# WKV recurrence with the distance to the past mean, two of its VectorE passes turned into ScalarE activations

## Chip, cores and metric

The kernel runs on one NeuronCore of a Trainium2 chip. The time is the device time in microseconds of one execution; medians are over repeated runs. PE is TensorE, DVE is VectorE, ACT is ScalarE, POOL is GpSimd, SP is SyncE.

## What is computed

Input x is 16 x 512 x 256 (8192 tokens, 256 channels), in fp32. After a layer norm there are two branches: `s`, an RWKV block (time mix and channel mix), and `g`, the SiLU of a mixture of 8 experts. The output is x + s * g. The part that the change touches is the time mix's recurrence:

```
def step(carry, kv_t):                  # one token, all channels
    aa, bb, pp = carry
    ww = u + kt
    p = jnp.maximum(pp, ww)
    e1 = jnp.exp(pp - p);  e2 = jnp.exp(ww - p)
    y = (e1 * aa + e2 * vt) / (e1 * bb + e2)
    ww2 = pp + w
    p2 = jnp.maximum(ww2, kt)
    e1 = jnp.exp(ww2 - p2);  e2 = jnp.exp(kt - p2)
    return ((e1 * aa + e2 * vt, e1 * bb + e2, p2), y)
rwkv = einsum(sigmoid(r) * y, Wo);  x = x + rwkv
```

Here w is minus the exponential of the decay parameter, u is `time_first`, and k, v, r are projections of the mixed tokens. The channel mix follows: relu squared of a 256 to 1024 projection, a projection back, gated by a sigmoid.

## The kernel before

The work has two stages. In the first, a round `b` takes one sequence of 512 tokens, channels on the partitions in two chunks `c` of 128 (`CH` = 2); there are 16 rounds, 0 to 15. In the second stage 72 tiles of 128 sorted tokens go through their expert.

Each engine has its own program with its instructions in an order written out by hand, and engines wait for each other on semaphores. An engine that waits holds up all that stands behind it in its program.

The recurrence is done by scans along the free dimension. In `wkv_start` DVE makes the running maximum `pp` (a scan), `qb` = pp - k, and in line 1317 the first exponent `E1` = min(qb + wneg, 0). ACT (`exponents`, `exps`) makes the second exponent `E2` with a Relu (line 562) and takes both exponentials (lines 566 and 568). `wkv_state` scans the denominator into `lb` (line 1323), `logs` takes its logarithm (line 574, with an ACT table load), `wkv_gap` adds it to `qb` (line 1330). `shares` then makes two tanh: that of the past in `E1` (line 580, with a table load) and that of now in `E2` (line 583). `wkv_mix` has seven DVE passes for each chunk: the share that is kept (line 1341), the fresh part (1344), the scan of the weighted mean `yy` (1348), 2v - mean (1353), and the three that join them and multiply by the receptance into `att` (1359, 1364, 1370).

A round of PE is, in order: `hidden(b-1)` (lines 845 to 852), `receptance(b-1)` in two halves (863), `channel_out(b-1, 0)` (875), `turn1(b+1)` (transposes, 780), `channel_out(b-1, 1)`, `project_out(b)` (827, reads `att`), `project(b+1, 0, 1)` (815, keys and values), `channel_out(b-1, 2)`, `turn2(b)`, `project(b+1, 2)`, `channel_out(b-1, 3)`. Between them stand small matmuls of the router.

ACT does in its round: the relus of `hidden` (596) and their squares (600), with `logs` after the second relu and `shares` after the sixth; then relus 6 and 7, three squares, the norm of the next sequence (510), two tanh (608), the affine after the transposes (518), copies of the projections (557, 555), the second norm (510), and at the end of the round for each chunk one copy, one exponent Relu (562) and one `split_mix` copy into `mix_hi` (589), then `exps`. The second half of `receptance` waits for relu 6, `channel_out(b-1, 0)` for all squares, `hidden(b)` for both copies into `mix_hi`.

On DVE `wkv_mix` is followed by a piece of routing work, `mix1(b+1)` (1277, 1282), `residual1` (1399, which waits for `project_out`; the second projection chunk of PE waits for it in turn), `wkv_start(b+1)`, `mix2` and `wkv_state` of the next round. In rounds 0 to 3 DVE also makes the router's statistics and softmax, in 11 it chooses the expert of each token, in 12 it places the tokens; from round 12 on POOL scatters list rows by indirect DMAs (line 400), which stand ahead of the scales of the next norm (lines 407 to 412) in its program.

Of the kernel before, what the change touches and what calls it, by code (L numbers as in the profile page):

```python
# [29 lines left out]
ALU = mybir.AluOpType  # L30
ACT = mybir.ActivationFunctionType
# [3 lines left out]
P = 128  # L35
# [6 lines left out]
WKV_STEPS = 16  # L42
PARAMS = ["ln1_w", "ln1_b", "ln2_w", "ln2_b", "decay", "first", "tmk", "tmv", "tmr", "cmk", "cmr"]


# [23 lines left out]
def rwkv_times_moe(nc, x, xT, vec, ln0_w, ln0_b, WkT, WvT, WrT, WoT, WfkT, WfrT, WfvT, Wg, W1, W2,  # L69
                   consts, tile_iota, token_ids, pad_rows, sorted_list, xs_rows, out):  # L70
    T, C = x.shape
    SEQ = 512
    NB = T // SEQ
    CH = C // P
    J = SEQ // P
# [3 lines left out]
    E, _, F = W1.shape  # L79
# [9 lines left out]
    with ExitStack() as ctx:  # L89
        def sb(name, shape, dt=F32):  # L90
            return ctx.enter_context(nc.sbuf_tensor(name, shape, dt))
# [7 lines left out]
        V = {n: i for i, n in enumerate(PARAMS)}  # L99
        wneg = sb("wneg", [P, CH])  # L100
        half_w = sb("half_w", [P, CH])
        half_u = sb("half_u", [P, CH])
        w0_bc = sb("w0_bc", [P, C])
        b0_bc = sb("b0_bc", [P, C])
# [42 lines left out]
        yy = [part(SEQ + 1) for _ in range(CH)]  # L147
# [6 lines left out]
        x_in = part(J * C).rearrange("p (j c) -> p j c", j=J)  # L154
# [67 lines left out]
        state_done log_done gap_done past_done now_done  # L222
# [5 lines left out]
        S = {n: sem(n) for n in names}  # L228
# [262 lines left out]
        def _(act):  # L491
# [67 lines left out]
            def exponents(b, c):  # L559

                wait_run(act, S["pre_done"], b * CH + (c + 1))
                act.activation(E2[:, c], qb[c], ACT.Relu, bias=wneg[:, c:c + 1]).then_inc(S["relu2_done"], 1)

            def exps(b):

                act.activation(E1, E1, ACT.Exp).then_inc(S["exp_done"], 1)
                wait_run(act, S["relu2_done"], b * CH + CH)
                act.activation(E2, E2, ACT.Exp, scale=-1.0).then_inc(S["exp_done"], 1)

            def logs(b):  # L570
# [5 lines left out]
            def shares(b):  # L576

                for c in range(CH):
                    wait_run(act, S["gap_done"], b * CH + (c + 1))
                    act.activation(E1[:, c], qb[c], ACT.Tanh, scale=-0.5, bias=half_w[:, c:c + 1]  # L580
                                   ).then_inc(S["past_done"], 1)
                for c in range(CH):
                    act.activation(E2[:, c], qb[c], ACT.Tanh, scale=-0.5, bias=half_u[:, c:c + 1]
                                   ).then_inc(S["now_done"], 1)
# [396 lines left out]
        def _(v):  # L981

            v.memset(hT[:, :, 0:1], 0.0)
            for c in range(CH):
                v.memset(pp[c][:, 0:1], -1e38)
                v.memset(lb[c][:, 0:1], 0.0)
                ins = v.memset(yy[c][:, 0:1], 0.0)
            ins.then_inc(S["columns_set"], 1)
            v.wait_ge(S["columns_set"], 1)

            def decay_parts():
                v.wait_ge(S["decay_exp"], 1)
                v.tensor_scalar(half_w[:], wneg[:], 0.5, None, ALU.mult)
                v.tensor_scalar(wneg[:], wneg[:], -1.0, None, ALU.mult)
                v.tensor_scalar(half_u[:], vecs[:, :, V["first"]], 0.5, None, ALU.mult)

            def prepare():
                v.wait_ge(S["weights_in"], 16 * 4)
                v.tensor_scalar(wo.rearrange("p k n -> p (k n)"), wo.rearrange("p k n -> p (k n)"), 0.125, None, ALU.mult)
# [304 lines left out]
            def wkv_start(b):  # L1304

                st = Steps(v, S["wkv_step"], WKV_STEPS, b, S["waited"])
                for c in range(CH):
                    v.wait_ge(S["kvr_ready"], b * (3 * CH) + (c + 1))
                    st.then(v.tensor_tensor_scan(pp[c][:, 1:SEQ + 1], wneg[:, c:c + 1].to_broadcast([P, SEQ]),
                                                 kvs[:, 0, c, :], -1e38, ALU.add, ALU.max))  # L1310
                for c in range(CH):
                    st.wait(1 + c)
                    st.then(v.tensor_tensor(qb[c], pp[c][:, 0:SEQ], kvs[:, 0, c, :], ALU.subtract))

                for c in range(CH):
# [16 lines left out]
            def wkv_mix(b):  # L1332

                st = Steps(v, S["wkv_step"], WKV_STEPS, b, S["waited"])
                st.k = 2 * CH
                val, r = kvs[:, 1], kvs[:, 2]
                v.wait_ge(S["kvr_ready"], b * (3 * CH) + 3 * CH)
                kept, fresh = [], []
                for c in range(CH):
                    wait_run(v, S["past_done"], b * CH + (c + 1))  # L1340
                    kept.append(st.then(v.tensor_scalar(pp[c][:, 1:SEQ + 1], E1[:, c], -0.5, 0.5, ALU.mult, ALU.add)))
                for c in range(CH):
                    st.wait(kept[c])
                    fresh.append(st.then(v.scalar_tensor_tensor(E1[:, c], E1[:, c], 1.0, val[:, c], ALU.add, ALU.mult)))
                means = []
                for c in range(CH):
                    st.wait(fresh[c])
                    means.append(st.then(v.tensor_tensor_scan(yy[c][:, 1:SEQ + 1], pp[c][:, 1:SEQ + 1], E1[:, c],
                                                              0.0, ALU.mult, ALU.add)))
                news = []  # L1350
                for c in range(CH):
                    st.wait(means[c])
                    news.append(st.then(v.scalar_tensor_tensor(val[:, c], val[:, c], 2.0, yy[c][:, 0:SEQ],
                                                               ALU.mult, ALU.subtract)))
                wait_run(v, S["now_done"], b * CH + CH)
                steps_to = []
                for c in range(CH):
                    st.wait(news[c])
                    steps_to.append(st.then(v.scalar_tensor_tensor(E2[:, c], E2[:, c], 1.0, val[:, c],
                                                                   ALU.add, ALU.mult)))  # L1360
                sums = []
                for c in range(CH):
                    st.wait(steps_to[c])
                    sums.append(st.then(v.scalar_tensor_tensor(E2[:, c], yy[c][:, 0:SEQ], 2.0, E2[:, c],
                                                               ALU.mult, ALU.add)))
# [227 lines left out]
```

## Time and profile before

| | before |
|---|---|
| median of 3 runs | 1146.2 us (1146.09 to 1147.34) |
| profiled execution | 1145.82 us, of which its span is 1144.0 us |
| busy share of the span: PE, DVE, ACT, POOL | 92%, 77%, 55%, 31% |
| first stage (rounds) | up to about 850 us |
| one of the rounds 5 to 10 | 47.5 us |
| granted TensorE clock, mean | 0.98 of full speed |

The span is from the first to the last instruction of the profile. Busy shares are means over stages with different limits; idle time of an engine counts only where another one waits for its result. A row with [t <-engine tile line] had t us of idle time on its engine just ahead of it, which that instruction ended. Rows with a count merge several instructions; their time is from the start of the first to the end of the last.

### The profile page before, as it was taken

What the parts mean: (1) busy time and instruction counts of PE and PEld (TensorE: products, weight loads), DVE (VectorE), ACT (ScalarE), POOL (GpSimd) and SP (SyncE); (2) the same over time, 40 slices, a digit from 0 to 9 for tenths busy, and PEclk for the clock granted to TensorE, in tenths of its full rate; (3) what the DMA queues carried; (4) which work ended last, traced back from release to release, by engine and by line L of the source; (5) the groups of instructions that cost most, each with busy time, mean ns of one, the idle gap of its engine ahead of it and who ended that gap; (6) DMA issues with size and microseconds to landing.
All of it is one profiled execution on the core that took longest, in us unless ns stands there. A gap on an engine that the chain in (4) does not pass through costs nothing.

```text
span 1144.0 us, 19481 instructions
## 1 busy us (share of the span) xinstructions
PE 1056.0 (92%) x5152; PEld 835.4 (73%) x5153; DVE 878.3 (77%) x1988; ACT 627.6 (55%) x1085; POOL 353.9 (31%) x403
## 2 busy tenths in 40 slices
PE   5689999999999999999998698989899999999997
PEld 5358777677766777767775577667788888888886
DVE  5899797988989889898898868786426666666664
ACT  2647466685765857658574557647333333433332
POOL 3122313100001000010000537364406555555563
PEclk9889999999999999999999899999999999999999
DMA  9422230110101101011010101053503333323220
GB/s 305 159 89 93 92 110 0 38 47 10 55 0 55 55 0 55 0 55 55 1 56 1 56 1 56 1 184 107 204 19 107 91 95 97 102 90 97 88 75 15
DMA packets 60054, 80.44 MB, mean 70 GB/s; under 512 B 7774, under 2 KB 47327, under 8 KB 60002
## 3 DMA queue, kind: packets, MB, share of 16 engines
q1 hardware_dynamic: 48658, 54.69, 14.7%
q0 software_dynamic: 11360, 25.32, 7.3%
q8 instruction: 17, 0.28, 0.1%
q14 instruction: 19, 0.16, 0.0%
HBM read 65.17 MB, written 26.49 MB: 80 GB/s over the span
## 4 chain that ended last, share of the span: by engine, by line
PE 55%; DVE 14%; issue 14%; ACT 11%; POOL 4%; DMA 1%; DVEq 1%; ACTq 0%; SPq 0%; POOLq 0%
PE psM L946 11%; PE psM L815 11%; PE psKV L875 11%; PE psM L957 5%; PE psR L957 5%; ACT arena L596 3%; PE psM L827 3%; DVE arena L1282 2%; POOL sorted_list L400 2%; PE psT L780 2%; ACT arena L600 2%; PE psT L936 2%; PE psR L736 2%; ACT L580 1%; ACT L574 1%
## 5 line engine op out<-in xcount | busy, mean ns | idle before, releaser
L875 PE MATMUL psKV<-arena 128*128 128x256 f32 x1024 | 236.0, 384 | 3.4 <-ACT arena L600 1.7
L875 PEld LDWEIGHTS psKV<-arena 128*128 128x128 f32 x1024 | 193.8, 192 | 42.6 <-issue 14.8
L815 PE MATMUL psM<-arena 128*128 128x512 f32 x384 | 174.2, 600 | 1.0
L407 POOL TENSOR_SCALAR lnw<-mv 128x4 f32<-128x4 f32 x32 | 8.8, 275 | 484.5 <-DVE mv L1263 484.3
L946 PE MATMUL psM<-arena 128*128 128x128 f32 x1152 | 144.3, 279 | 0.1
L946 PEld LDWEIGHTS psM<-arena 128*128 128x128 f32 x1152 | 135.8, 193 | 4.2 <-issue 1.8
L690 ACT ACTIVATE arena<-arena,info_t 128x256 f32<-128x256 f32 x72 | 43.1, 600 | 161.9 <-DVE info_t L1441 153.6
L815 PEld LDWEIGHTS psM<-arena 128*128 128x128 f32 x384 | 70.7, 192 | 81.7 <-issue 80.1
L467 POOL DMA_INDIRECT out_dram<-arena,out_idx x72 | 88.5, 1229 | 95.8 <-DVE row_idx L1436 81.9
L1282 DVE SCALAR_TENSOR_TENSOR arena<-arena,vecs 128x512 f32<-128x512 f32 x160 | 108.7, 746 | 0.0
L845 PE MATMUL psM<-mix_hi,wfk_hi 128*128 128x512 f32 x256 | 103.6, 405 | 2.5 <-ACT mix_hi L589 1.3
L510 ACT ACTIVATE arena<-s_ring,cf 128x256 f32 (+1 forms) x128 | 66.3, 591 | 68.0 <-POOL cf L412 68.0
L400 POOL DMA_INDIRECT sorted_list<-info_cur,place_cur x64 | 71.1, 1111 | 97.5 <-DVE info_cur L1239 78.6
L557 ACT ACTIVATE arena<-psM 128x512 f32<-128x512 f32 x64 | 36.5, 588 | 115.6 <-PE psM L815 115.6
L847 PE MATMUL psM<-mix_hi,wfk_lo 128*128 128x512 f32 x256 | 99.9, 390 | 0.0
L596 ACT ACTIVATE arena<-psM 128x512 f32<-128x512 f32 x128 | 74.1, 590 | 38.2 <-PE psM L852 38.0
L863 PE MATMUL psM<-arena 128*128 128x256 f32 x256 | 64.5, 396 | 24.5 <-ACT arena L596 24.5
L518 ACT ACTIVATE arena<-psT,vecs 128x512 f32<-128x512 f32 x64 | 46.4, 774 | 68.6 <-PE psT L780 68.6
L1507 DVE COPY arena<-arena 128x1024 f32 x72 | 50.4, 700 | 43.7 <-issue 41.7
L1277 DVE TENSOR_TENSOR arena<-arena 128x512 f32<-128x512 f32 x64 | 42.6, 692 | 53.3 <-ACT arena L518 53.3
L852 PE MATMUL psM<-mix_lo,wfk_hi 128*128 128x512 f32 x256 | 79.2, 390 | 0.7 <-DVE mix_lo L1301 0.7
L600 ACT ACTIVATE arena<-arena 128x512 f32<-128x512 f32 x128 | 77.1, 626 | 0.0
(191 smaller groups left out, 2006.4 us busy)
## 6 DMA issues: line engine op xcount, KB each, us to landing
desk<-in_x SPq DMA_DIRECT2D x16, 512.0 KB, 5.0
arena<-in_x SPq DMA_DIRECT2D x16, 512.0 KB, 3.8
desk<-in_xT SPq DMA_DIRECT2D x16, 512.0 KB, 4.1
xs_rows<-s_ring SPq DMA_DIRECT2D x16, 512.0 KB, 3.2
xs_rows<-in_x SPq DMA_DIRECT2D x16, 512.0 KB, 4.3
desk<-in_W SPq DMA_DIRECT2D x8, 512.0 KB, 8.3
arena<-in_W SPq DMA_DIRECT2D x8, 512.0 KB, 7.5
out_dram<-arena,out_idx POOLq DMA_INDIRECT x72, 2.8
```

What stands on the lines that cost most here:

```text
L400: pool.indirect_dma_start(sorted_list[:, :], bass.IndirectOffsetOnAxis(place_cur[:, j:j + 1], axis=0), info_cur[:, j, :], None).then_inc(S ...
L467: pool.indirect_dma_start(out[:, :], bass.IndirectOffsetOnAxis(out_idx[i][:, 0:1], axis=0), out_t[i], None, bounds_check=T - 1, oob_is_err ...
L596: act.activation(kf2[:, h], psM[:, h % 3, :], ACT.Relu).then_inc(S["relu_done"], 1)
L600: act.activation(kf2[:, h], kf2[:, h], ACT.Square).then_inc(S["sq_done"], 1)
L815: ins = pe.matmul(psM[:, u % 3, :], w[:, k, c * P:(c + 1) * P], mixA[:, m, k, :], start=(k == 0), stop=(k == CH - 1))
L845: pe.matmul(psM[:, h % 3, :], wfk_hi[:, k, n], mix_hi[:, k, :], start=(k == 0), stop=False)
L847: pe.matmul(psM[:, h % 3, :], wfk_lo[:, k, n], mix_hi[:, k, :], start=False, stop=False)
L852: ins = pe.matmul(psM[:, h % 3, :], wfk_hi[:, k, n], mix_lo[:, k, :], start=False, stop=(k == CH - 1))
L875: ins = pe.matmul(psKV[:, j // 2, (j % 2) * C:(j % 2 + 1) * C], kf2[:, h, j * P:(j + 1) * P], wfv[:, h, :], start=(h == 0), stop=(h == HC ...
L946: ins = pe.matmul(psM[:, i % 2, f * P:(f + 1) * P], w1_t[i % 2][:, k, f * P:(f + 1) * P], xnT[i % 2][:, k, :], start=(k == 0), stop=(k == ...
L957: ins = pe.matmul(y_ps[i % 2], hT_t[i % 2][:, f, :], w2_sb[:, ds(w + f * C, C)], start=(f == 0), stop=(f == FK - 1))
L1282: ins = v.scalar_tensor_tensor(dst[:, c], dmix[:, c], vecs[:, c, V[m]:V[m] + 1], hT[:, c, 0:SEQ], ALU.mult, ALU.add)
```

## The change

The recurrence is written with the distance of the token's value to the mean of the past: `wkv_mix` takes differences of neighbouring values and scans them into `lb`, weighted by the kept share; five DVE passes for each chunk instead of seven. The kept share is made by ACT from the past tanh (`kept_done`), ahead of the tanh of now. The first exponent is made in two steps by ACT, as Relu(wpos - qb) and a negative scale in the exponential, instead of line 1317 on DVE. `yy` goes, `x_in` takes its place in SBUF, two small constants (`wpos`, `half_c`) are added, and the scale of `wo` becomes 0.25.

```
             def exponents(b, c):
                 wait_run(act, S["pre_done"], b * CH + (c + 1))
                 act.activation(E2[:, c], qb[c], ACT.Relu, bias=wneg[:, c:c + 1]).then_inc(S["relu2_done"], 1)
+                act.activation(E1[:, c], qb[c], ACT.Relu, scale=-1.0, bias=wpos[:, c:c + 1]).then_inc(S["relu2_done"], 1)
             def exps(b):
-                act.activation(E1, E1, ACT.Exp).then_inc(S["exp_done"], 1)
-                wait_run(act, S["relu2_done"], b * CH + CH)
+                wait_run(act, S["relu2_done"], b * (2 * CH) + 2 * CH)
+                act.activation(E1, E1, ACT.Exp, scale=-1.0).then_inc(S["exp_done"], 1)
                 act.activation(E2, E2, ACT.Exp, scale=-1.0).then_inc(S["exp_done"], 1)
...
             def shares(b):
...
                     act.activation(E1[:, c], qb[c], ACT.Tanh, scale=-0.5, bias=half_w[:, c:c + 1]
                                    ).then_inc(S["past_done"], 1)
+                for c in range(CH):
+                    wait_run(act, S["past_done"], b * CH + (c + 1))
+                    act.activation(pp[c][:, 1:SEQ + 1], E1[:, c], ACT.Identity, scale=-0.5, bias=half_c[:, 0:1]
+                                   ).then_inc(S["kept_done"], 1)
                 for c in range(CH):
                     act.activation(E2[:, c], qb[c], ACT.Tanh, scale=-0.5, bias=half_u[:, c:c + 1]
                                    ).then_inc(S["now_done"], 1)
...
             def wkv_start(b):
...
-                    st.then(v.tensor_tensor(qb[c], pp[c][:, 0:SEQ], kvs[:, 0, c, :], ALU.subtract))
-
-                for c in range(CH):
-                    st.wait(3 + c)
-                    v.tensor_scalar(E1[:, c], qb[c], wneg[:, c:c + 1], 0.0, ALU.add, ALU.min).then_inc(S["pre_done"], 1)
+                    v.tensor_tensor(qb[c], pp[c][:, 0:SEQ], kvs[:, 0, c, :], ALU.subtract).then_inc(S["pre_done"], 1)
...
             def wkv_mix(b):
...
-                    kept.append(st.then(v.tensor_scalar(pp[c][:, 1:SEQ + 1], E1[:, c], -0.5, 0.5, ALU.mult, ALU.add)))
...
-                    fresh.append(st.then(v.scalar_tensor_tensor(E1[:, c], E1[:, c], 1.0, val[:, c], ALU.add, ALU.mult)))
...
-                    news.append(st.then(v.scalar_tensor_tensor(val[:, c], val[:, c], 2.0, yy[c][:, 0:SEQ],
-                                                               ALU.mult, ALU.subtract)))
+                for c in range(CH):
+                    wait_run(v, S["kept_done"], b * CH + (c + 1))
+                    steps.append(st.then(v.tensor_tensor(E1[:, c, 1:SEQ], val[:, c, 1:SEQ], val[:, c, 0:SEQ - 1],
+                                                         ALU.subtract)))
...
+                    dist.append(st.then(v.tensor_tensor_scan(lb[c][:, 1:SEQ + 1], pp[c][:, 0:SEQ], E1[:, c],
+                                                             0.0, ALU.mult, ALU.add)))
...
+                    back.append(st.then(v.scalar_tensor_tensor(E2[:, c], E2[:, c], -1.0, lb[c][:, 1:SEQ + 1],
+                                                               ALU.add, ALU.mult)))
...
+                    sums.append(st.then(v.scalar_tensor_tensor(E2[:, c], val[:, c], 2.0, E2[:, c],
                                                                ALU.mult, ALU.add)))
```

## Rows read from the trace of the kernel before

**Rows 1.** page, section 1: busy time of each engine

```profile
PE 1056.0 (92%) x5152; PEld 835.4 (73%) x5153; DVE 878.3 (77%) x1988; ACT 627.6 (55%) x1085; POOL 353.9 (31%) x403
```

**Rows 2.** waits of the matmul engine over the span (total us, times, longest us)

```profile
PE psM L863 <- ACT arena L596: 24.5, 13, 5.3
```

**Rows 3.** timeline of ACT in round 8 (start, duration, line, tiles, count)

```profile
439.38 1.33 ACT L580 ACTIVATE arena<-arena,half_w 128x512 f32<-128x512 f32 x2
440.62 1.32 ACT L583 ACTIVATE arena<-arena,half_u 128x512 f32<-128x512 f32 x2
441.84 1.06 ACT L596 ACTIVATE arena<-psM 128x512 f32<-128x512 f32 x2
442.80 1.66 ACT L600 ACTIVATE arena<-arena 128x512 f32<-128x512 f32 x3
...
449.29 1.45 ACT L518 ACTIVATE arena<-psT,vecs 128x512 f32<-128x512 f32 x2 [1.90 <-PE psT L780]
```

**Rows 4.** timeline of PE in round 8

```profile
442.47 1.99 PE L863 MATMUL psM<-arena 128*128 128x256 f32 x8 [1.52 <-ACT arena L596]
444.60 3.69 PE L875 MATMUL psKV<-arena 128*128 128x256 f32 x16
...
456.05 7.50 PE L815 MATMUL psM<-arena 128*128 128x512 f32 x16
```

**Rows 5.** timeline of PE in round 13

```profile
714.27 7.03 PE L815 MATMUL psM<-arena 128*128 128x512 f32 x16
```

**Rows 6.** timeline of DVE in round 8

```profile
441.03 0.76 DVE L1341 TENSOR_SCALAR arena<-arena 128x512 f32<-128x512 f32 x2
...
445.16 1.27 DVE L1353 SCALAR_TENSOR_TENSOR arena<-arena 128x512 f32<-128x512 f32 x2
...
451.62 1.29 DVE L1277 TENSOR_TENSOR arena<-arena 128x512 f32<-128x512 f32 x2
...
456.80 1.21 DVE L1399 TENSOR_TENSOR s_ring<-s_ring,psM 128x1024 f32 x1
```

**Rows 7.** groups of instructions: the first exponent on DVE

```profile
L1317 DVE TENSOR_SCALAR arena<-arena,wneg 128x512 f32<-128x512 f32 x32 | 14.0, 479 | 0.0
```

**Rows 8.** timelines of ACT, DVE and PE at the end of round 8

```profile
472.19 0.71 ACT L562 ACTIVATE arena<-arena,wneg 128x512 f32<-128x512 f32 x1
472.81 0.62 ACT L589 ACTIVATE mix_hi<-arena 128x512 fp32r<-128x512 f32 x1
...
475.35 2.34 DVE L1323 TENSOR_TENSOR_SCAN arena<-arena 128x512 f32<-128x512 f32 x2 [1.10 <-ACT arena L568]
...
474.96 0.48 PE L845 MATMUL psM<-mix_hi,wfk_hi 128*128 128x512 f32 x1
```

**Rows 9.** timeline of PE: waits of the other rounds

```profile
86.04 0.47 PE L845 MATMUL psM<-mix_hi,wfk_hi 128*128 128x512 f32 x1 [0.51 <-ACT mix_hi L589]
...
204.73 1.99 PE L863 MATMUL psM<-arena 128*128 128x256 f32 x8 [1.78 <-ACT arena L596]
...
610.03 2.07 PE L768 MATMUL psR<-desk,cst 128*128 128x512 f32 x2 [4.09 <-DVE desk L1170]
...
706.46 1.06 PE L780 MATMUL psT<-cst,arena 128*128 128x128 f32 x8 [1.50 <-ACT arena L510]
...
802.36 3.72 PE L827 MATMUL psM<-arena 128*128 128x256 f32 x16 [1.44 <-DVE arena L1370]
```

**Rows 10.** timeline of POOL in round 13

```profile
689.16 1.09 POOL L400 DMA_INDIRECT sorted_list<-info_cur,place_cur  x1 [15.52 <-DVE info_cur L1239]
```

**Rows 11.** timeline of PE around a stall in the expert stage

```profile
856.09 1.95 PE L946 MATMUL psM<-arena 128*128 128x128 f32 x16
...
862.09 0.44 PE L936 MATMUL psT<-cst,arena 128*128 128x128 f32 x2 [2.32 <-ACT arena L690]
862.36 3.52 PE L946 MATMUL psM<-arena 128*128 128x128 f32 x16
```

**Rows 12.** window after that stall (busy us by engine, PEclk, DMA share, GB/s)

```profile
862.60:863.00 0.40, 0.40 (x4) 0.40 (x3) 0.40 (x3) 0.28 (x1) 0.40 (x1) 0.50 0.70 236
```

More of the change, by code:

```diff
@@ L41 @@
 R_PEXP, R_COUNTS, R_SEL, R_ONEHOT, R_KEPT, R_ALL = 9, 13, 18, 30, 31, 54
-WKV_STEPS = 16
+WKV_STEPS = 10
 PARAMS = ["ln1_w", "ln1_b", "ln2_w", "ln2_b", "decay", "first", "tmk", "tmv", "tmr", "cmk", "cmr"]
@@ L101, in rwkv_times_moe @@
         half_w = sb("half_w", [P, CH])
+        wpos = sb("wpos", [P, CH])
+        half_c = sb("half_c", [P, 1])
         half_u = sb("half_u", [P, CH])
@@ L146, in rwkv_times_moe @@
         lb = [part(SEQ + 1) for _ in range(CH)]
-        yy = [part(SEQ + 1) for _ in range(CH)]
+        x_in = part(J * C).rearrange("p (j c) -> p j c", j=J)
         att = part(CH * SEQ).rearrange("p (c t) -> p c t", c=CH)
@@ L153, in rwkv_times_moe @@
         moe_end = at[0]
-        x_in = part(J * C).rearrange("p (j c) -> p j c", j=J)
         mixB_r = part(CH * SEQ).rearrange("p (c t) -> p c t", c=CH)
@@ L221, in rwkv_times_moe @@
         h1_ready mix1_step mix1_done mixr1_done proj_done kvr_ready wkv_step pre_done relu2_done exp_done att_done o_done
-        state_done log_done gap_done past_done now_done
+        state_done log_done gap_done past_done kept_done now_done
         x2_done ln2_step ln2_stats cf2_ready hn2_ready tr2_done h2_ready mix2_step mixk_done mixk_hi wfk_hi_done mix2_done mixr2_done
@@ L983, in _ @@
             v.memset(hT[:, :, 0:1], 0.0)
+            v.memset(half_c[:], 0.5)
             for c in range(CH):
                 v.memset(pp[c][:, 0:1], -1e38)
-                v.memset(lb[c][:, 0:1], 0.0)
-                ins = v.memset(yy[c][:, 0:1], 0.0)
+                ins = v.memset(lb[c][:, 0:1], 0.0)
             ins.then_inc(S["columns_set"], 1)
@@ L993, in decay_parts @@
                 v.tensor_scalar(half_w[:], wneg[:], 0.5, None, ALU.mult)
+                v.tensor_copy(wpos[:], wneg[:])
                 v.tensor_scalar(wneg[:], wneg[:], -1.0, None, ALU.mult)
@@ L998, in prepare @@
                 v.wait_ge(S["weights_in"], 16 * 4)
-                v.tensor_scalar(wo.rearrange("p k n -> p (k n)"), wo.rearrange("p k n -> p (k n)"), 0.125, None, ALU.mult)
+                v.tensor_scalar(wo.rearrange("p k n -> p (k n)"), wo.rearrange("p k n -> p (k n)"), 0.25, None, ALU.mult)
                 v.tensor_scalar(wfv.rearrange("p k n -> p (k n)"), wfv.rearrange("p k n -> p (k n)"), 0.5, None,
@@ L1334, in wkv_mix @@
                 st = Steps(v, S["wkv_step"], WKV_STEPS, b, S["waited"])
-                st.k = 2 * CH
+                st.k = CH
                 val, r = kvs[:, 1], kvs[:, 2]
                 v.wait_ge(S["kvr_ready"], b * (3 * CH) + 3 * CH)
-                kept, fresh = [], []
+                steps = []
                 for c in range(CH):
-                    wait_run(v, S["past_done"], b * CH + (c + 1))
-                    kept.append(st.then(v.tensor_scalar(pp[c][:, 1:SEQ + 1], E1[:, c], -0.5, 0.5, ALU.mult, ALU.add)))
+                    wait_run(v, S["kept_done"], b * CH + (c + 1))
+                    steps.append(st.then(v.tensor_tensor(E1[:, c, 1:SEQ], val[:, c, 1:SEQ], val[:, c, 0:SEQ - 1],
+                                                         ALU.subtract)))
@@ L1342, in wkv_mix @@
+                dist = []
                 for c in range(CH):
-                    st.wait(kept[c])
-                    fresh.append(st.then(v.scalar_tensor_tensor(E1[:, c], E1[:, c], 1.0, val[:, c], ALU.add, ALU.mult)))
-                means = []
-                for c in range(CH):
-                    st.wait(fresh[c])
-                    means.append(st.then(v.tensor_tensor_scan(yy[c][:, 1:SEQ + 1], pp[c][:, 1:SEQ + 1], E1[:, c],
-                                                              0.0, ALU.mult, ALU.add)))
@@ L1350, in wkv_mix @@
-                news = []
-                for c in range(CH):
-                    st.wait(means[c])
-                    news.append(st.then(v.scalar_tensor_tensor(val[:, c], val[:, c], 2.0, yy[c][:, 0:SEQ],
-                                                               ALU.mult, ALU.subtract)))
[L1355 to L1360, printed above, removed]
+                    st.wait(steps[c])
@@ new lines, in wkv_mix @@
+                    dist.append(st.then(v.tensor_tensor_scan(lb[c][:, 1:SEQ + 1], pp[c][:, 0:SEQ], E1[:, c],
+                                                             0.0, ALU.mult, ALU.add)))
+                wait_run(v, S["now_done"], b * CH + CH)
+                back = []
+                for c in range(CH):
+                    st.wait(dist[c])
+                    back.append(st.then(v.scalar_tensor_tensor(E2[:, c], E2[:, c], -1.0, lb[c][:, 1:SEQ + 1],
+                                                               ALU.add, ALU.mult)))
@@ L1361, in wkv_mix @@
                 sums = []
                 for c in range(CH):
-                    st.wait(steps_to[c])
-                    sums.append(st.then(v.scalar_tensor_tensor(E2[:, c], yy[c][:, 0:SEQ], 2.0, E2[:, c],
+                    st.wait(back[c])
+                    sums.append(st.then(v.scalar_tensor_tensor(E2[:, c], val[:, c], 2.0, E2[:, c],
                                                                ALU.mult, ALU.add)))
```

## The prediction

> **What bounds the kernel now.** I read the shares on the page first. PE is busy for 92% [rows 1], so only its idle time can be won, and any new idle time of PE is lost. The next view is the list of PE's waits. Beside waits at the kernel's ends, the largest group is the matmul of `receptance` (L863) that waits for ACT's relu (L596): 24.5 us in 13 waits, the longest 5.3 [rows 2], one in each of the rounds 3 to 15.
>
> Then one round's timelines, round 8, which stands for the rounds 4 to 10 (47.5 us each). ACT runs without a pause from the past tanh over the now tanh, relus 6 and 7, three squares and on to the norm [rows 3]. PE's second half of `receptance` starts at 442.47, after 1.52 us idle, just when relu 6 is done (442.3 to 442.4), and `channel_out` at 444.60, just after the last square (442.80 + 1.66 = 444.46) [rows 3, 4]. So this stretch of ACT's chain is on the path. PE then runs on to `project`, whose 16 matmuls take 7.50 us; in round 13, where `residual1` isn't late, they take 7.03 [rows 4, 5]. The 0.47 us are the second wait of the round: `residual1` starts at 456.80, after `mix1`, though PE was done with `project_out` at about 456.05 [rows 4, 6]. That one belongs to DVE.
>
> **The sum, part by part.** All is counted against the profiled execution's 1145.8 us; the median is 0.4 higher.
>
> *DVE's removed passes.* Kept share: two passes, 441.03 to the start of the next group at 441.70, 0.67 us. The fresh part is replaced by a subtraction of the same size, at nothing. 2v - mean: two of 0.6 each, 1.19. The first exponent: two passes of 0.48, some 0.8 with their overlap [rows 6, 7]. That is 2.65 us a round off DVE, but two other things set when DVE's results are used. `mix1` (L1277, at 451.62) needs the affine of ACT (L518, 449.29 to 450.74 for both chunks), which comes later by what ACT is delayed, and `residual1` needs `project_out`. In rounds 4 to 10 the whole worth of the relief is the 0.47 us of `project`; it comes back in full, since `mix1` starts no later than 451.5 and `residual1` then starts when `project_out` ends.
>
> *ACT's added Identity passes.* Two of 128x512, ahead of the tanh of now, so ahead of relus 6 and 7 and the squares. The trace has no Identity of this shape from SBUF with a bias operand. The nearest rows: tanh with a bias starts every 0.62 us (439.38, 440.62, 441.84 with two each); a square without a bias every 0.52 (442.80 to 444.35 with three); the affine from PSUM, with two operands, 1.45 for two, at most 0.7 each [rows 3]. Bounds 1.04 to 1.4 a round; I take the tanh's, 1.24, since source, size and bias are alike. They need no wait: the tanh before them is done. All of it lands on PE, since relu 6 and the last square were both last to come. Queued behind them on ACT are also the norm and the affine of the next sequence, later by 1.24 like PE itself.
>
> *ACT's added Relus*, one for each chunk at the end of the round, 0.62 each (L562 at 472.19, next start 472.81). The second copy into `mix_hi` ended at 473.43 and `hidden` started at 474.96 [rows 8]. So 1.24 of the 1.5 us of cover are used up, and I cost it at nothing; without cover it would be up to 1.24 a round. The exponentials end later too, so DVE's scan (475.35) starts about 1.1 later. In rounds 4 to 10 DVE catches up in its wait for the logarithm; in rounds 12 to 14 it isn't hidden, since PE waits there for the norm (706.46, 1.50), whose scales stand on POOL behind DMAs that start on what DVE copies after that scan (689.16, after 15.52 idle) [rows 9, 10].
>
> *Round by round.*
> - Round 0: DVE ahead of `project_out` gains 1.0 (1.86 less 0.85 from later exponentials), but `hidden` waited there for `mix_hi` already (86.04, 0.51) [rows 9], which comes 1.2 later: +0.2 (an estimate from the same passes).
> - Rounds 1 and 2: no wait of `project` to give back: +1.24 each, 2.5.
> - Round 3: its `project` gives back 0.26: +1.0.
> - Rounds 4 to 10: 7 x (1.24 - 0.47) = +5.4.
> - Round 11: PE waits 4.09 for DVE's choice (610.03) [rows 9]. DVE comes to `residual1` 0.5 later, since `project_out` is later by 1.24 and it had been late by 0.7: +0.5.
> - Rounds 12 to 14: POOL's start, 1.1 each: +3.3. The 1.24 on ACT vanishes in the wait for the norm.
> - Round 15: PE waited 1.44 for `att` (802.36) [rows 9]; DVE's shorter mix takes that away, and ACT's 1.24 takes its place: -0.2.
>
> Together +12.7 us from the instruction times alone: 1158.5 in this execution's terms, 1158.9 as a median. With the Identity's bounds it is 11 to 14.
>
> *The clock.* Each of these stalls grows: 1.52 to 2.8 us in the rounds 4 to 10, 1.78 (204.73, the same in 13 to 15) to 3.0 [rows 9]. None of those up to 1.78 is followed by a lower clock. The one stall in the trace that lies near the new length, 2.32 us at 862.09 in the expert stage, is: the granted clock is 0.50 in the window after it, which is the 1.2 GHz level, and 16 matmuls that took 1.95 us before take 3.52, so 1.57 are lost [rows 11, 12]. The 4.09 us of round 11 also cost a fall. Whether one of 2.8 brings a fall each time the rows can't say; one row for it, none of its length against it; the 12 stalls up to 1.78 are shorter. I take half of the ten stalls whose loss would reach PE's end (3 to 11 and 15; in 13 and 14 the wait for the norm hides most): 5 x 1.57 = +7.9, with bounds 0 and 10 x 1.57 = 15.7. Sum: 12.7 + 7.9 = 20.6, so 1166.4, as a median **1166.8**.
>
> The Trainium skill (TensorE: Matmul & The Clock Gate, A second HAM failure mode: psum-queue depth-cycling) says that a PE that idles briefly and often between its groups goes back and forth between the two clocks and loses throughput. By that, all ten would come and the time would be near 1174. The 12 stalls up to 1.78 disagree with it, the one of 2.32 agrees.
>
> The same notes (ScalarE: Activation LUTs, Rules for kernel authors) say to put relu, add and multiply on VectorE, not on ScalarE, which speaks against this change. The rows agree: the kept share takes 0.33 us a chunk on DVE, a pass with a bias 0.62 on ACT.
>
> **Rivals.**
> - *The clock stays up* (a stall of 2.8 isn't enough, or falls into a good moment nearly always): 12.7 alone, about 1159. For it: seven rounds with 1.5 idle each keep the clock. Chance 0.24.
> - *It falls nearly each time*: 12.7 + 15.7 = 28.4, so 1174 to 1175. Chance 0.11.
> - *ACT's passes are hidden and DVE's relief counts*: faster. ACT has idle time in each round (1.90 ahead of L518 [rows 3]), and if relu 6 weren't held up, DVE would give 7 x 0.47, 0.3 in round 3, 1.0 in round 0, about 0.7 in round 11 and up to 1.4 in round 15: 6.7, so 1139.5. It decides from an Identity cost below 0.24 us each (0.47 a round for two); the shortest ACT row of this size takes 0.52. Chance 0.04.
> - *Within 0.2%*: the same with the Identity at about 0.3 each. Chance 0.03.
>
> **How the numbers follow.** Half of the falls, give or take three of them (1162 to 1172), holds 0.58. A measurement of this kernel tells 0.2%, 2.3 us, from no change. Range: from the case without falls, at the Identity's lower bound (1157), to nearly all falls (1175); outside are left about 0.13. Faster 0.04, within 0.2% 0.03, slower 0.93.
>
> **What would show it.** In the profile after: two Identity rows of about 0.62 between the tanh of L580 and of now; PE's wait for L596 at 2.7 to 3.1 us in rounds 3 to 10; `project` at 7.0 us; rounds 4 to 10 at 48.3 us without a fall and 49.9 with one; a granted clock of 0.5 for some matmuls of `channel_out` in about half of the rounds. DVE's busy time falls by some 40 us (2.65 x 16) and ACT's rises by about 45 (four passes of 0.71 x 16). It would be wrong if PE's wait for relu 6 stays at 1.5 (the Identities hidden), if `hidden` begins to wait for `mix_hi` (the Relus not hidden), or if the clock does other than half.

## The result

| | before | after |
|---|---|---|
| median | 1146.77 us (1146.09 to 1148.85, 4 runs) | 1169.58 us (1166.86 to 1175.80, 4 runs) |
| profiled execution, its span | 1145.82, 1144.0 us | 1170.22, 1168.4 us |
| mean granted TensorE clock | 0.98 | 0.97 |

The ratio is 1.0203 (95%: 1.016 to 1.0247): the change makes the kernel 2% slower. The forecast was 1166.8 us.

Page of the kernel after, busy time of each engine:

```profile
PE 1067.1 (91%) x5152; PEld 843.5 (72%) x5153; DVE 839.2 (72%) x1892; ACT 665.4 (57%) x1149; POOL 356.6 (31%) x403
```

Against [rows 1] DVE has 39.1 us less to do and ACT 37.8 more, so the work has moved as written. PE has the same number of matmuls and is busy for 11.1 us longer: some of them ran slower. The other 13.3 us of the longer span (24.4) are new idle time of PE, in sum over all its waits.

Waits of PE in the kernel after (total us, times, longest us):

```profile
PE psM L869 <- ACT arena L602: 43.7, 15, 7.5
...
PE psM L833 <- DVE arena L1366: 3.3, 1, 3.3
...
PE psM L851 <- ACT mix_hi L595: 2.4, 2, 1.6
```

The matmul of `receptance` (now L869) waits for the relus (now L602) for 43.7 us where it was 24.5 [rows 2]. No other group of waits grew like it; taken together the others shrank by 5.9 us. Where this comes from is in the timeline of ACT in round 7 of the kernel after (round 8 in [rows 3]; the rounds 4 to 10 are alike):

```profile
404.64 1.33 ACT L582 ACTIVATE arena<-arena,half_w 128x512 f32<-128x512 f32 x2
405.88 1.32 ACT L586 ACTIVATE arena<-arena,half_c 128x512 f32<-128x512 f32 x2
407.10 1.32 ACT L589 ACTIVATE arena<-arena,half_u 128x512 f32<-128x512 f32 x2
408.33 1.05 ACT L602 ACTIVATE arena<-psM 128x512 f32<-128x512 f32 x2
409.29 1.66 ACT L606 ACTIVATE arena<-arena 128x512 f32<-128x512 f32 x3
...
439.34 0.71 ACT L564 ACTIVATE arena<-arena,wpos 128x512 f32<-128x512 f32 x1
439.95 0.62 ACT L595 ACTIVATE mix_hi<-arena 128x512 fp32r<-128x512 f32 x1
```

The chain is still without a pause, and the two Identity passes (L586) take 1.22 us of it, from 405.88 to 407.10. Relu 6 starts 3.69 us after the past tanh, where it was 2.46. PE in the same round:

```profile
408.96 2.00 PE L869 MATMUL psM<-arena 128*128 128x256 f32 x8 [2.78 <-ACT arena L602]
411.09 3.71 PE L881 MATMUL psKV<-arena 128*128 128x256 f32 x16
...
422.57 7.11 PE L821 MATMUL psM<-arena 128*128 128x512 f32 x16
...
441.13 0.48 PE L851 MATMUL psM<-mix_hi,wfk_hi 128*128 128x512 f32 x1
```

The stall grew from 1.52 to 2.78 us. `project` takes 7.11 where it took 7.50 [rows 4], and `hidden` starts without a wait: the Relus (L564) are covered here. DVE in this round:

```profile
416.61 1.36 DVE L1284 TENSOR_TENSOR arena<-arena 128x512 f32<-128x512 f32 x2 [1.03 <-ACT arena L519]
...
422.83 1.22 DVE L1395 TENSOR_TENSOR s_ring<-s_ring,psM 128x1024 f32 x1 [0.89 <-PE psM L833]
```

DVE is now early: `residual1` (L1395) waited 0.89 us for `project_out`. What DVE gained beyond the 0.39 of `project` it spends waiting.

Round 5 shows the second part of the loss, the clock. PE's timeline, and below it four windows of it (busy us of PE, PEld, DVE, ACT and POOL, then PEclk, DMA share, GB/s):

```profile
310.73 2.76 PE L869 MATMUL psM<-arena 128*128 128x256 f32 x8 [2.78 <-ACT arena L602]
...
313.29 4.59 PE L881 MATMUL psKV<-arena 128*128 128x256 f32 x16
```

```profile
310.70:311.70 1.00, 0.97 (x4) 0.86 (x5) 1.00 (x2) 1.00 (x3) 0.00 (x0) 1.00 1.05 292
311.90:312.90 1.00, 1.00 (x4) 0.73 (x4) 1.00 (x3) 1.00 (x3) 0.00 (x0) 0.50 0.96 280
312.90:313.90 1.00, 1.00 (x4) 0.82 (x3) 1.00 (x3) 1.00 (x3) 0.00 (x0) 0.50 0.42 107
315.30:316.30 1.00, 1.00 (x6) 0.86 (x6) 0.70 (x5) 0.35 (x1) 0.00 (x0) 1.00 0.24 84
```

The same stall of 2.78 us, but a good microsecond after its end the granted clock is 0.50 (the 1.2 GHz level), and it is back at 2.4 GHz at 315.30. The two groups of matmuls take 7.35 us together instead of 5.71. Of the 15 rounds from 1 on, this profile shows such a fall after the stall in 3, 5, 8, 11, 13 and 14 (in 12, where a longer wait ends, before had one too).

Where the 24.4 us of span lie, from the times at which the same instructions start in the two profiles:

| stretch | longer by | made of |
|---|---|---|
| start to `hidden(0)` (86.04 to 88.53) | 2.5 | 0.5 ahead of `project_out(0)`, 0.9 of lower clock in it, 1.08 longer wait for `mix_hi` |
| to the stall of round 3 (204.73 to 212.28) | 5.1 | 3 x 1.24 and one fall (in round 0, after `hidden`) |
| to the stall of round 11 (585.07 to 604.10) | 11.5 | 8 x 0.92 and three falls at 1.30 |
| to the stall of round 12 (643.16 to 666.68) | 4.5 | 1.24, DVE late by 2.0, one fall |
| to the end | 0.9 | nearly all hidden |

In the rounds 4 to 10 a round without a fall takes 48.46 us (47.54 before) and one with a fall 49.76.

The first row of the table needs more than the page. In round 0 DVE's scan has to wait for the exponentials (L570), which in the kernel before were done when it started at 42.77; PE waits longer for DVE's next result (L742, 7.54 us where it was 6.48), and then less for `att` (L833, 3.26 where it was 5.13). DVE and PE of the kernel after, and `project_out(0)` of the kernel before:

```profile
45.17 2.34 DVE L1326 TENSOR_TENSOR_SCAN arena<-arena 128x512 f32<-128x512 f32 x2 [1.90 <-ACT arena L570]
...
50.93 3.56 PE L742 MATMUL psR<-desk 128*128 128x8 f32 x16 [7.54 <-DVE desk L1041]
...
64.28 6.27 PE L833 MATMUL psM<-arena 128*128 128x256 f32 x16 [3.26 <-DVE arena L1366]
```

```profile
63.76 5.39 PE L827 MATMUL psM<-arena 128*128 128x256 f32 x16 [5.13 <-DVE arena L1370]
```

The 16 matmuls of `project_out(0)` take 0.9 us longer because the clock, which is low there in both kernels, rises later: between 67.30 and 69.00 it is 0.50 in the kernel after and 1.00 in the kernel before.

### The profile page after: what moved, and what is told of

It reads as the page before. It is cut to its first block, busy times and chain, and to the rows that moved or that the text cites. A ratio compares the mean times of both kernels' runs of the same rounds, so it can differ in the third digit from the quotient of the medians.

```text
span 1168.4 us, 19401 instructions
## 1 busy us (share of the span) xinstructions
PE 1067.1 (91%) x5152; PEld 843.5 (72%) x5153; DVE 839.2 (72%) x1892; ACT 665.4 (57%) x1149; POOL 356.6 (31%) x403
## 4 chain that ended last, share of the span: by engine, by line
PE 68%; ACT 14%; issue 9%; DVE 4%; POOL 4%; DMA 1%; ACTq 0%; SPq 0%; POOLq 0%; DVEq 0%
PE psKV L881 17%; PE psM L821 13%; PE psM L952 11%; PE psM L963 5%; PE psR L963 5%; PE psM L833 5%; ACT arena L602 3%; PE psM L869 3%; PE psT L786 3%; POOL sorted_list L401 2%; PE psT L942 2%; PE psR L742 2%; ACT L582 1%; ACT L576 1%; ACT arena L606 1%
## 5 line engine op out<-in xcount | busy, mean ns | idle before, releaser
L881 PE MATMUL psKV<-arena 128*128 128x256 f32 x1024 | 242.3, 390 | 2.7 <-ACT arena L606 1.7
L881 PEld LDWEIGHTS psKV<-arena 128*128 128x128 f32 x1024 | 198.3, 197 | 44.2 <-issue 13.2
L952 PEld LDWEIGHTS psM<-arena 128*128 128x128 f32 x1152 | 134.3, 192 | 4.5 <-issue 2.1
L821 PEld LDWEIGHTS psM<-arena 128*128 128x128 f32 x384 | 71.7, 193 | 78.7 <-issue 77.9
L468 POOL DMA_INDIRECT out_dram<-arena,out_idx x72 | 92.6, 1287 | 91.2 <-DVE row_idx L1432 76.4
L869 PE MATMUL psM<-arena 128*128 128x256 f32 x256 | 70.0, 421 | 43.7 <-ACT arena L602 43.7
L869 PEld LDWEIGHTS psM<-arena 128*128 128x128 f32 x256 | 50.4, 205 | 56.8 <-ACT arena L602 49.8
L602 ACT ACTIVATE arena<-psM 128x512 f32<-128x512 f32 x128 | 74.2, 591 | 26.1 <-PE psM L858 26.1
```

Of the source, the lines that this page charges most:

```text
L468: pool.indirect_dma_start(out[:, :], bass.IndirectOffsetOnAxis(out_idx[i][:, 0:1], axis=0), out_t[i], None, bounds_check=T - 1, oob_is_err ...
L602: act.activation(kf2[:, h], psM[:, h % 3, :], ACT.Relu).then_inc(S["relu_done"], 1)
L821: ins = pe.matmul(psM[:, u % 3, :], w[:, k, c * P:(c + 1) * P], mixA[:, m, k, :], start=(k == 0), stop=(k == CH - 1))
L869: ins = pe.matmul(psM[:, (HC + u) % 3, (j % 2) * C:(j % 2 + 1) * C], mixB_r[:, k, j * P:(j + 1) * P], wfr[:, k, :], start=(k == 0), stop=( ...
L881: ins = pe.matmul(psKV[:, j // 2, (j % 2) * C:(j % 2 + 1) * C], kf2[:, h, j * P:(j + 1) * P], wfv[:, h, :], start=(h == 0), stop=(h == HC ...
L952: ins = pe.matmul(psM[:, i % 2, f * P:(f + 1) * P], w1_t[i % 2][:, k, f * P:(f + 1) * P], xnT[i % 2][:, k, :], start=(k == 0), stop=(k == ...
```

## The experiments

Eleven runs were made, in three groups, each group on one chip. There the kernel before took 1155 to 1160 us instead of 1147. In its one profile from there (before_again) the rounds 4 to 10 take 47.54 us as in the first, and 7.3 of the 9.0 us that its span is longer lie behind the stall of round 15, nearly all of that in the expert stage. So each kernel is read as a ratio to the kernel before on its own chip.

| kernel | median us | before there | ratio (95%) | rounds 4 to 10, no fall |
|---|---|---|---|---|
| kept_act | 1177.28 | 1159.89 | 1.0163 (1.0139 to 1.0188) | |
| exp_act | 1166.66 | 1159.89 | 1.0074 (1.0052 to 1.0097) | 47.71 |
| dist_only | 1155.22 | 1159.89 | 0.9959 (0.9941 to 0.9977) | 47.23 |
| filled | 1175.01 | 1159.89 | 1.0147 (1.0129 to 1.0165) | 48.44 |
| after_again | 1178.84 | 1154.58 | 1.0214 (1.0196 to 1.0232) | |
| now_late | 1157.27 | 1154.58 | 1.0011 (1.0000 to 1.0022) | 47.30 |
| dist_now_late | 1142.06 | 1154.58 | 0.9886 (0.9868 to 0.9903) | 46.35 |
| before_now_late | 1155.43 | 1154.58 | 1.0007 (0.9995 to 1.0018) | 47.54 |
| before_again | 1154.83 (one execution) | 1155.38 | | 47.54 |
| exp_again | 1162.27 | 1155.38 | 1.0069 (1.0050 to 1.0088) | 47.71 |
| kept_one | 1159.02 | 1155.38 | 1.0034 (1.0022 to 1.0047) | 47.78 |

### The three parts, each alone

**kept_act**: the kernel before, with only the kept share on ACT.

```
                                    ).then_inc(S["past_done"], 1)
+                for c in range(CH):
+                    wait_run(act, S["past_done"], b * CH + (c + 1))
+                    act.activation(pp[c][:, 1:SEQ + 1], E1[:, c], ACT.Identity, scale=-0.5, bias=half_c[:, 0:1]
+                                   ).then_inc(S["kept_done"], 1)
...
-                    wait_run(v, S["past_done"], b * CH + (c + 1))
-                    kept.append(st.then(v.tensor_scalar(pp[c][:, 1:SEQ + 1], E1[:, c], -0.5, 0.5, ALU.mult, ALU.add)))
...
+                    wait_run(v, S["kept_done"], b * CH + (c + 1))
```

> The kernel before with the kept share alone made by ACT (two Identity passes ahead of the tanh of now); DVE makes six passes per chunk, the first exponent stays on DVE. Theory (the Identities push relu 6 and the last square, and the longer stall brings clock falls): PE's wait for relu 6 grows from 1.5 to 2.8 us in rounds 4 to 10, a round there from 47.5 to 48.4; +10 to 11 us from the instruction times and about five falls of 1.3, so +14 to +20, about 1164. Rival (the cost sits in the Relus of the exponent and the later exponentials): +4 or less, under 1151.

**exp_act**: the kernel before, with only the first exponent on ACT (a Relu for each chunk, a negative scale in the exponential).

```
                 act.activation(E2[:, c], qb[c], ACT.Relu, bias=wneg[:, c:c + 1]).then_inc(S["relu2_done"], 1)
+                act.activation(E1[:, c], qb[c], ACT.Relu, scale=-1.0, bias=wpos[:, c:c + 1]).then_inc(S["relu2_done"], 1)
...
-                    st.wait(3 + c)
-                    v.tensor_scalar(E1[:, c], qb[c], wneg[:, c:c + 1], 0.0, ALU.add, ALU.min).then_inc(S["pre_done"], 1)
```

> The kernel before with the first exponent alone moved to ACT (two Relus at the end of the round, line 1317 gone). Theory: in rounds 1 to 11 the Relus hide behind PE (cover of 1.5 us ahead of hidden, 1.24 used), so nothing there; about +1.2 in round 0 where hidden waits for mix_hi, +1.1 in each of rounds 12 to 14 through POOL's start: +3 to +6, about 1151, and no new stall of PE above 1.8 us in rounds 3 to 10. Rival (half of the loss comes from here): +10 or more, and PE waits for mix_hi in every round.

**dist_only**: the kernel after, with the kept share and the first exponent back on DVE; only the new form of the recurrence is left.

```
-                for c in range(CH):
-                    wait_run(act, S["past_done"], b * CH + (c + 1))
-                    act.activation(pp[c][:, 1:SEQ + 1], E1[:, c], ACT.Identity, scale=-0.5, bias=half_c[:, 0:1]
-                                   ).then_inc(S["kept_done"], 1)
...
-                    wait_run(v, S["kept_done"], b * CH + (c + 1))
+                    wait_run(v, S["past_done"], b * CH + (c + 1))
+                    kept.append(st.then(v.tensor_scalar(pp[c][:, 1:SEQ + 1], E1[:, c], -0.5, 0.5, ALU.mult, ALU.add)))
```

> The changed kernel with the kept share and the first exponent back on DVE, so the new recurrence alone, which takes one pass per chunk (1.2 us a round) off DVE and adds nothing to ACT. Theory: project no longer waits for residual1 in rounds 4 to 10 (7 x 0.4), round 0 and round 15 gain 1.2 each, round 11 some 0.7: -5 to -7, about 1140, with PE's wait for relu 6 at 1.5 as before. Rival (DVE off the path altogether): within 1 us of before. Rival (DVE is the bound of the round): -1.2 x 15 = -18.

Measured: kept_act +18.7 us (1.63% of 1146.8), exp_act +8.5, dist_only -4.7. They sum to 22.5, where the whole gave 23.3 and, as after_again, 24.5; each of the three is known to some 2 to 3 us by its interval, so the sum fits. So the kept share on ACT is most of the loss, and the new form by itself is a small gain. kept_act and dist_only came out about as expected (dist_only a little short of its 5 to 7), exp_act cost more than the 3 to 6 us expected. PE in round 5 of kept_act, with the clock window after it:

```profile
306.74 3.37 PE L868 MATMUL psM<-arena 128*128 128x256 f32 x8 [2.77 <-ACT arena L601]
```

```profile
307.00:308.00 1.00, 1.00 (x3) 0.82 (x4) 1.00 (x2) 1.00 (x3) 0.00 (x0) 0.50 0.94 227
```

The stall is the same as in the kernel after, so it comes from the Identities alone. The clock fell after 10 of the 12 long stalls (rounds 3 to 11 and 13 to 15), more often than in the kernel after and twice as often as I had expected for this run. PE in round 5 of dist_only:

```profile
300.97 2.00 PE L864 MATMUL psM<-arena 128*128 128x256 f32 x8 [1.51 <-ACT arena L597]
...
314.59 7.11 PE L816 MATMUL psM<-arena 128*128 128x512 f32 x16
```

Here the stall stays at 1.51, and the shorter DVE gives back what it can: `project` takes 7.11 instead of 7.50, and the round 0.31 less.

### Does the clock count apart from the stall?

**filled**: the kernel after, where PE does the first half of `receptance` twice, the second time in what was idle time. The matmuls that wait for relu 6 can't start sooner.

```
                     pe.wait_ge(S["relu_done"], b * HC + (HC + u - 2))
-                    for j in (2 * u, 2 * u + 1):
+                    for j in (0, 1, 0, 1) if u == 0 else (2, 3):
```

> The changed kernel in which PE makes the first half of receptance twice, the same 8 matmuls again into the same bank, 1.9 us of work set into the wait for relu 6 (which ends when it ended before). The instruction times stay, but PE is idle for 0.9 instead of 2.8 us; in rounds 1 and 2, where the wait is only 1.2, it costs 0.7 each. Theory (the long idle stretch of PE is what lowers the clock): no falls in rounds 3 to 10, a time 4 to 8 us below the changed kernel, about 1164, and the spread from run to run gets small. Rival (the falls have another cause): the falls stay and the time is 1 to 2 us above the changed kernel.

**after_again**: the kernel after once more, on another chip.

> The changed kernel itself, beside the three reorderings on one chip. Theory and rival alike: about 2% slower than before (1.016 to 1.025), with PE waiting 2.7 to 3.0 us for relu 6 in rounds 3 to 11 and a fall of the clock in some of them, not in the same rounds as in the first profile.

PE in round 5 of filled, with the clock window around it:

```profile
308.90 2.00 PE L869 MATMUL psM<-arena 128*128 128x256 f32 x8 [1.04 <-ACT arena L602]
```

```profile
308.00:310.00 2.00, 1.10 (x5) 1.00 (x6) 2.00 (x2) 2.00 (x5) 0.00 (x0) 1.00 1.02 314
```

The rounds take 48.44 us, those of the kernel after without a fall 48.46. So in these rounds the added matmuls cost nothing and gain nothing in instruction times. No stall of the rounds 3 to 11 and 13 to 15 is followed by a fall, and the ratio is 1.0147 instead of 1.0203 and 1.0214: 0.6 to 0.7%, 6 to 8 us, are the clock's. The spread between runs, which I had expected to shrink clearly, was 3.6 us in 5 runs, against 6.6 in 12 runs of the kernel before there and 4.6 in 5 runs of after_again; with so few runs it settles nothing. In after_again the clock fell after 8 of the 12 long stalls, in other rounds than in the first profile (4, 7 to 10 and 13 to 15).

### Undoing the order instead of the work

**now_late**: the kernel after, with ACT's tanh of now moved behind relus 6 and 7 and the squares. ACT does the same work.

```
+            def share_now(b):
                 for c in range(CH):
                     act.activation(E2[:, c], qb[c], ACT.Tanh, scale=-0.5, bias=half_u[:, c:c + 1]
...
                     relus(b - 1, 6, 7)
                     squares(b - 1, 5, 6, 7)
+                share_now(b)
```

> The changed kernel with one move: ACT makes relus 6 and 7 and the squares 5, 6, 7 before the tanh of now, so the same ACT passes, two of them later. Theory (what costs is that the Identities stand ahead of relu 6 and the squares): PE's wait for relu 6 is back at 1.5 us, no falls in rounds 3 to 10, a round there 47.2 us, and what is left of the loss is round 0 and rounds 12 to 14: 1.000 to 1.005 of before. Rival (ACT's total time or DVE's wait for the kept share costs): little changes, above 1.012.

**dist_now_late**: the same move in dist_only.

> The new recurrence with kept share and first exponent on DVE, and the tanh of now after the squares. Theory: the last square ends 1.24 us earlier than in the kernel before, the wait for relu 6 falls to 0.3, and with 1.2 us less on DVE mix1 keeps pace: rounds 4 to 10 at 46.2 to 46.4 us, 0.985 to 0.990 of before. Rival (PE's wait only moves elsewhere): 0.995 or more, as the new recurrence alone.

**before_now_late**: the same move in the kernel before.

> The kernel before with only that move of the tanh of now. Theory: PE gets 1.2 us earlier to project, but mix1 and residual1 on DVE end when they did, so the wait of project for residual1 grows from 0.5 to 1.6 us and eats it: within 0.3% of before, rounds at 47.4 to 47.6. Rival (ACT's order is all that counts): as much as the move gives elsewhere, 0.99 or less.

PE in the stall of round 5, in now_late, in dist_now_late and in before_now_late:

```profile
303.58 2.00 PE L872 MATMUL psM<-arena 128*128 128x256 f32 x8 [1.53 <-ACT arena L604]
```

```profile
294.71 2.00 PE L867 MATMUL psM<-arena 128*128 128x256 f32 x8 [0.32 <-ACT arena L599]
```

```profile
298.36 1.99 PE L866 MATMUL psM<-arena 128*128 128x256 f32 x8 [0.29 <-ACT arena L598]
...
315.27 5.39 PE L818 MATMUL psM<-arena 128*128 128x512 f32 x12 [1.36 <-DVE s_ring L1402]
```

In now_late, with every added pass still on ACT, the stall is back at 1.53, no clock falls in the rounds 3 to 10, and of the 2.1% there are 0.11% left. ACT's work is the same as in the kernel after, so what costs is how much of it stands ahead of relu 6, not how much ACT does in all. The added passes have not become free by the move: the Identities still stand ahead of relu 6, only the tanh of now doesn't. dist_now_late has the same order without the passes that were moved to ACT, and on the same chip it is 1.3% faster than now_late (1142.06 and 1157.27), with a stall of 0.32 us instead of 1.53 and rounds of 46.35 instead of 47.30. ACT's chain in round 8 of dist_now_late shows the order:

```profile
431.89 1.33 ACT L581 ACTIVATE arena<-arena,half_w 128x512 f32<-128x512 f32 x2
433.13 1.06 ACT L599 ACTIVATE arena<-psM 128x512 f32<-128x512 f32 x2
434.09 1.66 ACT L603 ACTIVATE arena<-arena 128x512 f32<-128x512 f32 x3
435.65 1.32 ACT L586 ACTIVATE arena<-arena,half_u 128x512 f32<-128x512 f32 x2
```

The last two kernels show DVE's side. In the kernel before the move takes 1.26 us off the stall, and PE then waits 1.36 for `residual1`: the time goes to DVE, and the round stays at 47.54. With the shorter `wkv_mix` the same move takes the round from 47.23 to 46.35, and the kernel to 0.9886 of the one before. Alone, the new form gave -0.4% and the move nothing; together they give -1.1%. This version beats both kernels.

### The exponent's share, and a smaller stall

**before_again** (the kernel before) and **exp_again** (exp_act) on one chip, to see where a change whose rounds are nearly unchanged (47.71) loses 0.7%.

> The kernel before, unchanged, for a profile taken on the same chip as the next two. Nothing is tested: its rounds 4 to 10 should take 47.5 us each as in the first profile, and what differs from that profile belongs to the chip.

> The first exponent alone moved to ACT, again, since it cost 8.6 us against 3 to 6 expected, and no profile of before from the same chip stood beside it. Theory: round by round against before's profile from this chip, about 1.2 in round 0, nothing to 0.2 in each of rounds 1 to 10, 1.1 to 1.3 in each of 12 to 14; 4 to 7 us in all. Rival (rounds 1 to 10 lose, since the cover ahead of hidden is gone): 0.5 or more in each of them.

PE at `hidden(0)`, in before_again and in exp_again:

```profile
87.02 0.47 PE L845 MATMUL psM<-mix_hi,wfk_hi 128*128 128x512 f32 x1 [0.51 <-ACT mix_hi L589]
```

```profile
89.46 0.47 PE L847 MATMUL psM<-mix_hi,wfk_hi 128*128 128x512 f32 x1 [1.59 <-ACT mix_hi L591]
```

Of 8.0 us of span, 2.4 are there already (1.08 of them this wait, and 1.0 a longer `project_out(0)`, whose clock rises later), about nothing comes in rounds 1 and 2, 0.15 a round up to 11 (1.2), 2.0 from 11 to 12 (half of it by the time DVE has made its choice, 611.03 to 615.71, half behind that, where DVE's scan waits for the exponentials, 625.43 to 631.10), 3.7 from 13 to 14, and 1.5 are won back at the end (7.8 together). The 3.7 hold a fall of the clock and a wait for the norm of 3.30 instead of 1.49. The other profile of this kernel, exp_act's, had only 0.95 there, but 1.5 from 14 to 15 where exp_again has none. What makes the two differ was not found.

**kept_one**: the kernel before with the kept share of only the first chunk on ACT, one Identity instead of two.

```
-                for c in range(CH):
+                for c in range(1):
                     wait_run(act, S["past_done"], b * CH + (c + 1))
                     act.activation(pp[c][:, 1:SEQ + 1], E1[:, c], ACT.Identity, scale=-0.5, bias=half_c[:, 0:1]
...
+                kept = st.then(v.tensor_scalar(pp[1][:, 1:SEQ + 1], E1[:, 1], -0.5, 0.5, ALU.mult, ALU.add))
```

The diff is against kept_act.

> The kernel before with the kept share of one chunk made by ACT and that of the other by DVE: one Identity instead of two ahead of relu 6. Theory: PE's wait for relu 6 is 2.1 to 2.2 us in rounds 4 to 10, between the 1.55 that never brought a fall of the clock there and the 2.8 that did in about every second; I expect a fall in at most two of these rounds, and 0.5 to 0.7% over before. Rival (the falls come with any longer wait): falls in half of the rounds, 0.9% or more.

PE in the stalls of rounds 3, 4 and 14 of kept_one, and the clock after the last two:

```profile
207.51 2.71 PE L868 MATMUL psM<-arena 128*128 128x256 f32 x8 [2.38 <-ACT arena L601]
...
256.82 2.00 PE L868 MATMUL psM<-arena 128*128 128x256 f32 x8 [2.15 <-ACT arena L601]
...
754.22 3.27 PE L868 MATMUL psM<-arena 128*128 128x256 f32 x8 [2.39 <-ACT arena L601]
```

```profile
256.80:260.00 3.20, 3.05 (x13) 2.42 (x14) 3.20 (x5) 3.20 (x7) 0.00 (x0) 1.00 0.84 273
754.20:757.00 2.80, 2.78 (x8) 2.28 (x9) 2.80 (x4) 2.01 (x4) 2.48 (x4) 0.60 1.05 313
```

The ratio is 1.0034, below what I expected. The seven stalls of 2.15 to 2.17 (rounds 4 to 10) and that of 1.95 in round 11 kept the clock, and the four of 2.37 to 2.39 (rounds 3, 13, 14 and 15) lost it. Half of the added passes cost a fifth of the 1.63%: without falls the price is 0.24 us a round, since DVE gives part back.

## Why the prediction was right, and where its terms were off

The direction, the mechanism and nearly the size were right: two passes on ACT ahead of relu 6, together 1.24 us each round (measured 1.22), DVE's relief worth only `project`'s wait, and a clock that falls after some of the longer stalls and not after others. kept_act and now_late show the first, dist_only and before_now_late the second, filled the third. Of the signs named these held: the Identities start 0.61 us apart, the stall is 2.74 to 2.97 in the rounds 3 to 10, `hidden` doesn't wait in the rounds 4 to 10, DVE's busy time fell by 39.1 us, and six of twelve stalls lost the clock. ACT's rose by 37.8 us and not by 45, since its 64 added passes took 0.59 us each on average and not 0.71. The rival of a clock that stays up is out, and so is that of hidden passes. That of a fall nearly each time nearly came in kept_act (10 of 12). The half was a choice between none and all for which the rows had one stall, and that stall keeps the clock in seven of the ten profiles that have it (last section); the kernel after itself lost the clock 8 times of 12 in after_again. That this term came so near is partly luck.

Point by point, against the profile's 24.4 us (forecast 20.6):

- *Rounds 4 to 10, instruction times.* Forecast +0.77, measured +0.92. The stall grew by 1.22 on average (1.55 to 2.76) and `project` gave back 0.39, not 0.47, since it takes 7.11 and not 7.03; 0.09 are elsewhere. Over the eight rounds 3 to 10 the forecast was 6.4 and 7.6 were measured, 1.2 us more.
- *Round 0.* Forecast +0.2, measured +2.5. The wait of `hidden(0)` grew by 1.08, about as worked out. DVE's gain ahead of `project_out(0)` came too, and more than forecast (PE's wait for `att` fell by 1.87), but PE came to that wait 2.4 later, a lateness that I had left out. 1.06 of it is PE's longer wait for DVE, whose scan waits for the later exponentials, and the same wait of 7.54 stands in exp_act and exp_again, so it comes with the Relus. 0.9 more are the later rise of the clock, which dist_only shows without the Relus (its `project_out(0)` takes 6.62): they aren't an instruction time.
- *Rounds 11 to 15.* Forecast 2.4 from the stall of round 11 on, measured 5.4, less a fall of 1.3: 4.1. In round 11 I let DVE gain 0.7; it lost 2.0 there, and 2.0 again in exp_again, half of it behind the later exponentials. For the rounds 12 to 14 I had 1.1 each through POOL's start. exp_again has 3.9 there in all and exp_act 2.9 (against before_again), near the forecast 3.3, but not as equal steps (0.1, 3.7 and 0 in exp_again), and no run tested the way through POOL.
- *The clock.* Forecast 5 falls at 1.57, 7.9. Measured: one in round 0, four in the rounds 3 to 11, at 1.30 each in the round's length, so 6.5, and with the 0.9 of `project_out(0)` 7.4; those of 13 and 14 are nearly hidden, as forecast. filled gives 6 to 8 us by another way.

So 12.7 of instruction times were 17.0 (24.4 - 7.4), and 7.9 of clock were 7.4. The Relus at the end of the round were the mis-sized term: costed at nothing in the rounds 1 to 10 and at some 4.5 us in the others, they are nearly covered in the rounds 1 to 10 but not in 0 and 11, and by themselves cost 0.7%, some 8 us.

The Trainium skill (TensorE: Matmul & The Clock Gate, A second HAM failure mode: psum-queue depth-cycling) says that a PE with frequent short idle times between its groups of matmuls goes back and forth between the two clocks. The prediction took it as a fall at each of the longer stalls; by the profiles it was 6, 8 and 10 of 12. The Trainium skill (ScalarE: Activation LUTs, Rules for kernel authors) says to put relu, add and multiply on VectorE. The runs agree in sign: each of the two moves to ACT made the kernel slower.

What stays open: the 0.09 us a round, the part of round 0's 2.4 that isn't the 1.06, the way in which the rounds 12 to 14 come to be late, and the 3.7 us between rounds 13 and 14 of exp_again.

## What to carry to other kernels

Moving a pass to an engine that is idle for 45% of the time isn't free: look at what stands behind it in that engine's program and who waits for that. Here the same passes made the kernel 2.1% slower; with another pair moved from ahead of PE's operand to behind it 0.1% was left, but against that same order without the passes it is still 1.3%. Relief on an engine pays only where it ends last; when two engines take turns as the last, try the two reliefs together (-0.4% and 0, but -1.1% together). And price a longer stall of PE for its clock too, not only for its length.

## What the runs showed of the hardware

Short stalls of the `receptance` matmul never lost the clock: not the 72 of 1.3 to 1.79 us (rounds 3 to 11 and 13 to 15 of before twice, exp_act twice, dist_only and now_late), not the one of 1.95, and not the seven of 2.15 to 2.17. The four of 2.37 to 2.39 each did. The seven are rounds of one kernel that follow each other at the same 47.78 us, so they count for less than seven separate trials.

There is no sharp step between 2.17 and 2.37, though. The first long stall of the expert stage, which the prediction read in [rows 11], is 2.30 to 2.34 us long in ten of the profiles. It lost the clock in three of them (before, now_late, kept_one) and kept it in seven. In before_again, the same kernel as in [rows 11], the same 16 matmuls take 1.95 us and not 3.52:

```profile
864.22 0.44 PE L936 MATMUL psT<-cst,arena 128*128 128x128 f32 x2 [2.32 <-issue]
864.49 1.95 PE L946 MATMUL psM<-arena 128*128 128x128 f32 x16
```

```profile
864.20:867.00 2.80, 2.78 (x22) 2.71 (x23) 2.05 (x8) 1.08 (x3) 2.19 (x3) 1.00 0.34 94
```

Among the 36 stalls of 2.5 to 3.0 us (kernel after twice, kept_act), 24 lost it and 12 didn't, and the same round differs from run to run: round 4 kept the clock in the first profile of the kernel after and lost it in after_again, round 5 the other way round, with the same stall of 2.74 to 2.78. So length alone doesn't decide. In the 24 the clock fell between 0.7 us before the stall's end and 1.4 us after it. What else decides no experiment tested; it stays open.
